# A recurrent step whose f gate takes the two halves of h in separate products

## The reference, cut to what matters

```
xW = einsum('ntd,dk->tnk', x, Wx) + b
def step(carry, xw_t):
    prev_h, prev_c = carry
    a = xw_t + prev_h @ Wh
    i = sigmoid(a[:, 0:Hdim]);          f = sigmoid(a[:, Hdim:2 * Hdim])
    o = sigmoid(a[:, 2 * Hdim:3 * Hdim]); g = tanh(a[:, 3 * Hdim:4 * Hdim])
    next_c = f * prev_c + i * g
    next_h = o * tanh(next_c)
    return (next_h, next_c), next_h
```

## Time and profile before

| what | value |
|---|---|
| time, median of 3 runs | 1904.62 us (1903.64 to 1904.72) |
| time of the profiled execution | 1905.15 us |
| its span, first to last instruction | 1903.0 us |
| TensorE clock granted, mean over the span | 0.626 of full |
| start of the first recurrent step | 468 us |
| last step alone from about | 1590 us |
| busy: TensorE, VectorE, ScalarE, GpSimd | 64%, 62%, 50%, 21% |

### The profile page before, as it was taken

How to read it: one execution, slowest core, us unless ns; L and a number is a source line. 1 busy time by engine, 2 the same in 40 slices (tenths; PEclk the granted TensorE clock), 3 DMA queues, 4 the chain that set the end, 5 groups by cost and what they waited for, 6 DMA issues and landing times.

```text
span 1903.0 us, 60748 instructions
## 1 busy us (share of the span) xinstructions
PE 1214.6 (64%) x21103; PEld 978.4 (51%) x21103; DVE 1174.1 (62%) x6657; ACT 950.6 (50%) x3287; POOL 404.2 (21%) x802
## 2 busy tenths in 40 slices
PE   4666677176777558867775588677764976444444
PEld 3544445145655445656554466555553665444443
DVE  6456634222777765657777666577776665666665
ACT  0333378234766644556666445466654554333332
POOL 4222234432221131311221312112114130000000
PEclk9667655588555557975555589655555886555555
DMA  8000000000000000000000000000000000000000
GB/s 257 0 0 0 0 1 0 1 1 1 3 0 0 2 3 2 2 25 3 0 1 3 2 2 2 25 2 0 1 2 3 2 2 13 0 0 0 0 0 13
DMA packets 14555, 17.85 MB, mean 9 GB/s; under 512 B 3348, under 2 KB 13208, under 8 KB 14360
## 3 DMA queue, kind: packets, MB, share of 16 engines
q1 hardware_dynamic: 10248, 10.50, 1.7%
q10 hardware_dynamic: 4112, 4.86, 0.9%
HBM read 13.25 MB, written 2.10 MB: 8 GB/s over the span
## 4 chain that ended last, share of the span: by engine, by line
PE 41%; DVE 25%; ACT 14%; issue 11%; POOL 6%; DMA 1%; POOLq 1%; ACTq 1%; DVEq 1%; SPq 0%
PE psum L727 20%; DVE cnew L1275 4%; DVE cadd L1272 4%; ACT tC L973 4%; DVE h L1283 3%; PE psum L701 3%; DVE h L1286 3%; PE psum L710 3%; DVE gO L1269 3%; PE psum L669 3%; POOL sc L226 3%; PE psum L679 2%; PE psum L559 2%; PE psum L596 2%; DVE h L1284 1%
## 5 line engine op out<-in xcount | busy, mean ns | idle before, releaser
L727 PE MATMUL psum<-h,wh 128*128 128x8 f16 x16384 | 514.6, 168 | 437.6 <-DVE h L1286 419.6
L727 PEld LDWEIGHTS psum<-h,wh 128*128 128x128 f16 x16384 | 479.7, 103 | 558.4 <-DVE h L1286 526.1
L967 ACT ACTIVATE tA<-gA 128x16 f32<-128x16 f32 x512 | 110.5, 216 | 474.5 <-DVE gA L1265 473.7
L1265 DVE TENSOR_REDUCE gA<-psum 128x16 f32<-128x32 f32 x512 | 97.4, 190 | 214.2 <-PE psum L727 213.5
L973 ACT ACTIVATE tC<-cnew 128x8 f32<-128x8 f32 x512 | 108.8, 213 | 130.9 <-DVE cnew L1275 87.3
L596 PE MATMUL psum<-qbd,kT 128*128 128x256 f16 x512 | 151.0, 400 | 24.5 <-ACT weights L853 21.5
L1272 DVE SCALAR_TENSOR_TENSOR cadd<-tA 128x8 f32<-128x8 f32 x512 | 126.8, 248 | 52.6 <-ACT tA L967 45.4
L853 ACT ACTIVATE weights<-psum 128x512 f16<-128x512 f32 x256 | 152.1, 594 | 0.0
L1283 DVE TENSOR_TENSOR h<-oU,tC 128x8 f16<-128x8 f32 x512 | 89.2, 174 | 97.1 <-ACT tC L973 96.3
L342 POOL TENSOR_TENSOR weights<-tmp,weights 128x512 f16<-128x512 f32 x64 | 74.0, 1157 | 313.2 <-ACT weights L853 313.2
L611 PEld LDWEIGHTS psum<-vs,weights 128*128 128x128 f16 x2048 | 112.3, 111 | 37.6 <-issue 17.2
(11 more groups left out here) (225 smaller groups left out, 2183.7 us busy)
## 6 DMA issues: line engine op xcount, KB each, us to landing
arena<-in_x_dram SPq DMA_DIRECT2D x4, 512.0 KB, 10.0
wf<-in_L_cond_w_f_dram SPq DMA_DIRECT2D x2, 1024.0 KB, 19.7
xs<-in_x_dram SPq DMA_DIRECT2D x4, 512.0 KB, 5.4
out_dram<-place SPq DMA_DIRECT2D x16, 128.0 KB, 2.1
arena<-in_L_cond_w_ada_dram ACTq DMA_DIRECT2D x1, 1536.0 KB
weights<-in_L_cond_Wh_dram ACTq DMA_DIRECT2D x1, 1024.0 KB, 14.7
gates<-in_L_cond_b_ada_dram ACTq DMA_DIRECT2D x8, 128.0 KB, 15.0
wx<-in_L_cond_Wx_dram SPq DMA_DIRECT2D x1, 1024.0 KB, 21.5
```

What stands on the lines that cost most here:

```text
L727: last = mm(cols, wh16[:, half, kc, (g0 + g) * P:(g0 + g + 1) * P], h16[:, kc, :, :], start=False, stop=g == n - 1 and kc == KD - 1 and ha ...
```

## The change

The high and low parts of h move to a new tile `hl`, in which each stands as the third of three columns, the first two being constants. The F bank gets one column per sequence instead of two. TensorE starts each step as soon as the high part is written: it multiplies it with the f gate's weights (8 matmuls of 4 columns). It then waits for the low part and runs gate A (16 matmuls of 8 columns), the low part's products of f into the same columns (8 of 4 columns), and gate O (8 of 8 columns). Since the F bank now holds finished sums, ScalarE reads it directly, the reduce `gF` goes, and the preload of bank F waits for ScalarE's tanh instead of it. On VectorE, h in fp32 is no longer formed for the low part: a scan over triples computes, from the constants, o, tanh(c) and the high part, first 1, then o, then o times tanh(c) minus the high part. It waits until the high part is written. The output store forms o times tanh(c) itself.

```diff
--- before.py
+++ after.py
@@ -157,18 +157,17 @@
         ot = place[:, B * D:2 * B * D]
         big1 = sb("big1", [P, 8])
 
-        h16 = sb("h16", [P, KD, B, 2], F16)
+        hl = sb("hl", [P, 2, KD, B, 3], F16)
         gA = sb("gA", [P, 16])
-        gF = sb("gF", [P, 8])
         gO = sb("gO", [P, 8])
-        h32 = sb("h32", [P, KD * B])
         tA = sb("tA", [P, 16])
         tO = sb("tO", [P, 8])
-        oU = sb("oU", [P, 8])
+        ot3 = sb("ot3", [P, KD * B, 3])
         cmul = sb("cmul", [P, 8, 3])
         cadd = sb("cadd", [P, 8, 3])
         cnew = sb("cnew", [P, 8, 3])
-        tC = sb("tC", [P, 8])
+        oU, tC = ot3[:, :, 1], ot3[:, :, 2]
+        hcol, hi3, lo3 = hl[:, 0, :, :, 2], hl[:, 0].rearrange("p k b e -> p (k b e)"), hl[:, 1].rearrange("p k b e -> p (k b e)")
         unit = sb("unit", [P, GC])
 
         psum = ctx.enter_context(nc.psum_tensor("psum", [P, 8, 512], F32))
@@ -281,11 +280,11 @@
 
         CHUNK = (0, 1, 6, 7, 2, 3, 4, 5)
         UNIT = (0.5,) * 2 + (1.0,) * 2 + (0.5,) * 4
-        GATE_BANKS = ((pA, 0, 4, "l_A"), (pF, 4, 2, "l_F"), (pO, 6, 2, "l_O"))
-
-        def gate_cols(bk, n, r):
-
-            return bk[:, r * n * B * 2:(r + 1) * n * B * 2].rearrange("p (c e) -> p c e", e=2)
+        GATE_BANKS = ((pA, 0, 4, 2), (pF, 4, 2, 1), (pO, 6, 2, 2))
+
+        def gate_cols(bk, n, e, r):
+
+            return bk[:, r * n * B * e:(r + 1) * n * B * e].rearrange("p (c e) -> p c e", e=e)
 
         WLOADS = 8
         BLOCK_LINKS = 105
@@ -704,29 +703,38 @@
                 if half == 1 and b % 2 == 0:
                     pe_gates_T(n + 1, b + 1)
 
-            def put_gates(bk, g0, n, first):
+            def put_gates(bk, g0, n, e, first):
 
                 part = (xw[:, first:first + ROUND, g0:g0 + n, :] if isinstance(first, int) else xw[:, bass.ds(first, ROUND), g0:g0 + n, :])
-                mm(bk[:, 0:ROUND * n * B * 2].rearrange("p (t c e) -> p t c e", t=ROUND, e=2)[:, :, :, 0], ident[:], part.rearrange("p t g b -> p t (g b)"),
+                mm(bk[:, 0:ROUND * n * B * e].rearrange("p (t c e) -> p t c e", t=ROUND, e=e)[:, :, :, 0], ident[:], part.rearrange("p t g b -> p t (g b)"),
                    start=True, stop=True, skip_group_check=True)
 
             def put_round(m, first):
 
-                for (bk, g0, n, made), read in zip(GATE_BANKS, ("l_gA", "l_gF", "l_gO")):
+                for (bk, g0, n, e), read in zip(GATE_BANKS, ("l_gA", "l_tF", "l_gO")):
                     pe.wait_ge(s[read], m)
-                    put_gates(bk, g0, n, first)
+                    put_gates(bk, g0, n, e, first)
+
+            def gate_products(which, r, h_of):
+
+                bk, g0, n, e = GATE_BANKS[which]
+                for g in range(n):
+                    cols = gate_cols(bk, n, e, r)[:, g * B:(g + 1) * B, :]
+                    for kc in range(KD):
+                        for half in range(2):
+                            last = mm(cols, wh16[:, half, kc, (g0 + g) * P:(g0 + g + 1) * P], h_of(kc),
+                                      start=False, stop=g == n - 1 and kc == KD - 1 and half == 1, skip_group_check=True)
+                return last
 
             def pe_step(m, r, more=True):
 
+                both = lambda kc: hl[:, :, kc, :, 2].rearrange("p e b -> p b e")
+                pe.wait_ge(s["l_hi"], m)
+                gate_products(1, r, lambda kc: hl[:, 0, kc, :, 2])
                 pe.wait_ge(s["l_lo"], m)
-                for bk, g0, n, made in GATE_BANKS:
-                    for g in range(n):
-                        cols = gate_cols(bk, n, r)[:, g * B:(g + 1) * B, :]
-                        for kc in range(KD):
-                            for half in range(2):
-                                last = mm(cols, wh16[:, half, kc, (g0 + g) * P:(g0 + g + 1) * P], h16[:, kc, :, :],
-                                          start=False, stop=g == n - 1 and kc == KD - 1 and half == 1, skip_group_check=True)
-                    last.then_inc(s[made], 1)
+                gate_products(0, r, both).then_inc(s["l_A"], 1)
+                gate_products(1, r, lambda kc: hl[:, 1, kc, :, 2]).then_inc(s["l_F"], 1)
+                gate_products(2, r, both).then_inc(s["l_O"], 1)
                 if r == ROUND - 1 and more:
                     put_round(m, m % (2 * P))
 
@@ -965,12 +973,12 @@
             def act_step(m, i, r):
                 act.wait_ge(s["l_gA"], m)
                 A(tA[:], gA[:], ACT.Tanh, scale=down).then_inc(s["l_tA"], 1)
-                act.wait_ge(s["l_gF"], m)
-                A(cmul[:, :, 1], gF[:], ACT.Tanh, scale=down).then_inc(s["l_tF"], 1)
+                act.wait_ge(s["l_F"], m)
+                A(cmul[:, :, 1], gate_cols(pF, 2, 1, r)[:, :, 0], ACT.Tanh, scale=down).then_inc(s["l_tF"], 1)
                 act.wait_ge(s["l_gO"], m)
                 A(tO[:], gO[:], ACT.Tanh, scale=down).then_inc(s["l_tO"], 1)
                 act.wait_ge(s["l_c"], m)
-                A(tC[:], cnew[:, :, 2], ACT.Tanh, scale=0.5).then_inc(s["l_tC"], 1)
+                A(tC, cnew[:, :, 2], ACT.Tanh, scale=0.5).then_inc(s["l_tC"], 1)
 
             act.wait_ge(s["l_init"], 2)
             for part in range(2):
@@ -1048,7 +1056,11 @@
 
             d.memset(qbd[:], 0.0).then_inc(s["l_init"], 1)
             d.memset(vs[:, :, :, :, HD:HD + 1], V_UP).then_inc(s["l_init"], 1)
-            d.memset(h16[:], 0.0).then_inc(s["l_lo"], 1)
+            d.memset(ot3[:], 0.0).then_inc(s["dinit"], 1)
+            d.memset(hl[:], 0.0).then_inc(s["dinit"], 1)
+            v.wait_ge(s["dinit"], 2)
+            d.memset(hl[:, 0, :, :, 0], -1.0).then_inc(s["l_hi"], 1)
+            v.sem_inc(s["l_lo"], 1)
             d.memset(cmul[:, :, 0], 0.0).then_inc(s["dinit"], 1)
             d.memset(cmul[:, :, 2], 0.5).then_inc(s["dinit"], 1)
             d.memset(cadd[:], 0.0).then_inc(s["dinit"], 1)
@@ -1056,7 +1068,7 @@
             d.memset(kap[:, NT:], 0.0).then_inc(s["dinit"], 1)
             d.memset(kmn[:, NT:], 0.0).then_inc(s["dinit"], 1)
 
-            v.wait_ge(s["dinit"], 6)
+            v.wait_ge(s["dinit"], 8)
             for k in range(NT):
                 if k % B == 0:
                     v.wait_ge(s[f"ld_x{k // B}"], 16)
@@ -1262,11 +1274,9 @@
             def dve_step(m, i, r):
 
                 v.wait_ge(s["l_A"], m)
-                d.tensor_reduce(gA[:], gate_cols(pA, 4, r), axis=AX.X, op=ALU.add).then_inc(s["l_gA"], 1)
-                v.wait_ge(s["l_F"], m)
-                d.tensor_reduce(gF[:], gate_cols(pF, 2, r), axis=AX.X, op=ALU.add).then_inc(s["l_gF"], 1)
+                d.tensor_reduce(gA[:], gate_cols(pA, 4, 2, r), axis=AX.X, op=ALU.add).then_inc(s["l_gA"], 1)
                 v.wait_ge(s["l_O"], m)
-                d.tensor_reduce(gO[:], gate_cols(pO, 2, r), axis=AX.X, op=ALU.add).then_inc(s["l_gO"], 1)
+                d.tensor_reduce(gO[:], gate_cols(pO, 2, 2, r), axis=AX.X, op=ALU.add).then_inc(s["l_gO"], 1)
 
                 v.wait_ge(s["l_tA"], m)
                 d.scalar_tensor_tensor(cadd[:, :, 2], tA[:, 0:8], 1.0, tA[:, 8:16], ALU.add, ALU.mult).then_inc(s["l_ig"], 1)
@@ -1275,19 +1285,17 @@
                 d.tensor_tensor_scan(cnew[:].rearrange("p c e -> p (c e)"), cmul[:].rearrange("p c e -> p (c e)"),
                                      cadd[:].rearrange("p c e -> p (c e)"), 0.0, ALU.mult, ALU.add).then_inc(s["l_c"], 1)
                 v.wait_ge(s["l_tO"], m)
-                d.tensor_scalar(oU[:], tO[:], 1.0, 0.5 * H_UP, ALU.add, ALU.mult).then_inc(s["l_oU"], 1)
+                d.tensor_scalar(oU, tO[:], 1.0, 0.5 * H_UP, ALU.add, ALU.mult).then_inc(s["l_oU"], 1)
                 v.wait_ge(s["l_tC"], m)
                 v.wait_ge(s["l_oU"], m)
-                hi, lo = (h16[:, :, :, half] for half in range(2))
-                by_k = lambda t: t[:].rearrange("p (k b) -> p k b", b=B)
-                d.tensor_tensor(hi, by_k(oU), by_k(tC), ALU.mult).then_inc(s["l_hi"], 1)
-                d.tensor_tensor(h32[:], oU[:], tC[:], ALU.mult).then_inc(s["l_h32"], 1)
-                v.wait_ge(s["l_h32"], m)
-                d.tensor_tensor(lo, by_k(h32), hi, ALU.subtract).then_inc(s["l_lo"], 1)
+                by_k = lambda t: t.rearrange("p (k b) -> p k b", b=B)
+                d.tensor_tensor(hcol, by_k(oU), by_k(tC), ALU.mult).then_inc(s["l_hi"], 1)
+                v.wait_ge(s["l_hi"], m + 1)
+                d.tensor_tensor_scan(lo3, ot3[:].rearrange("p c e -> p (c e)"), hi3, 0.0, ALU.mult, ALU.subtract).then_inc(s["l_lo"], 1)
                 d.tensor_copy(cadd[:, :, 0:2], cnew[:, :, 2:3].to_broadcast([P, KD * B, 2])).then_inc(s["l_cc"], 1)
 
-                d.tensor_copy(hs[:, :, :, i:i + 1] if isinstance(i, int) else hs[:, :, :, bass.ds(i, 1)],
-                              h32[:].rearrange("p (k b o) -> p k b o", b=B, o=1)).then_inc(s["l_hs"], 1)
+                d.tensor_tensor(hs[:, :, :, i:i + 1] if isinstance(i, int) else hs[:, :, :, bass.ds(i, 1)],
```

(7 more changed lines are left out.)

## The result

The changed kernel takes 1945.66 us (median; 1942.58 to 1947.17) where the kernel before takes 1904.13: a ratio of 1.0216, 95% interval 1.0199 to 1.0234. Slower, as forecast, but by 41.5 us and not by 7, and outside the forecast range of 1898 to 1925 us.

What follows compares the result with a forecast made beforehand. The prediction took a chain of hand-overs, no engine above 41% of it, as the bound. Losses of 15.5 and 2 us less a gain of 10.7 made +7 us on the median 1904.62: 1911.5 us, range 1898 to 1925.

Steps and rivals of the forecast that it cites:

- 8 x 0.0274 = 0.22 us of TensorE more: Per step on TensorE: splitting F turns 8 matmuls of 8 columns into 16 of 4, costing 0.22 us more.
- Rival 2: Tail: TensorE, carrying more matmuls, might be granted the higher clock; -13 us over 128 steps, 1899 us together; chance 0.05.
- Low part earlier by 0.035 us: VectorE: the scan ends the low part 0.242 us behind the high one, against 0.277; 10.7 us gained over 305 steps.
- F's first half fits under the scan: Where TensorE is idle: the eight matmuls are done at 0.27 us, gate A can start at 0.29, 0.02 to spare.
- The charge per matmul: TensorE: a matmul of 4 columns is charged the same 0.027 us as one of 8 columns.
- Late steps pay in full: Where TensorE comes late, gate A starts 0.20 to 0.22 us later, reaching the end in full: 74 x 0.21 = 15.5 us.
- Rival 1: Hardly anything is lost where TensorE is late: fewer than 33 of 74 steps pay; 1899 us with 25 paying; chance 0.12.
- Reduce of F gone, worth nothing: In an idle step, dropping F's reduce gains nothing: ScalarE's tanh of f is done 0.11 us before the scan of c.
- The sum: Whole kernel: 15.5 us for late steps plus 2 for 64 steps between, less 10.7 gained, together +7 us.

Runs made afterwards that it cites:

- e1: The changed kernel without the products of h's low half with the f gate's weights in the attention loop's steps; 1920.66 us, ratio 1.0071 to the kernel before.
- e2: The kernel before with 8 unread matmuls of 4 columns more in each step of the attention loop's body; 1919.62 us, ratio 1.0070.
- e8: The changed kernel with TensorE's attention loop of three turns written out as straight code; 1928.28 us, ratio 1.0125 to the kernel before.
- e7: The kernel before with 8 unread matmuls of 4 columns more in each carried step outside the attention loop's body; 1932.09 us, ratio 1.0126.
- e0: The changed kernel run once more, unaltered; 1947.15 us, ratio 1.0209 to the kernel before.
- e3: The changed kernel with F kept whole and its reduce, leaving the low part's scan and the product for hs; 1902.59 us, ratio 0.9983 to the kernel before.
- e5: The changed kernel with F's split and ScalarE's direct read only in the tail's 128 steps, the scan in all; 1901.00 us, ratio 0.9969 to the kernel before.
- e9: As e5, but the tail's step behind each preload keeps F whole with its reduce; 1898.38 us, ratio 0.9966 to the kernel before.

## Why the prediction was wrong

**Where it failed: what the eight matmuls cost.** The prediction charged splitting F with "8 x 0.0274 = 0.22 us of TensorE more", and with nothing else. That term is right for TensorE's own time. Two further prices hang on the same eight.

- *Their instructions.* The attention loop's body grew from 1513 to 1769 profiled instructions. The prediction never asked whether a loop body still fits, nor did a rival. It cost 18.3 us, shown by e1, e2 and e8. The trace of before had a sign of it: ten instruction pieces in 465 to 640 us, none in the last two turns of the loop. Where the limit lies it did not tell. The Trainium skill (Runtime: NRT & Kernel Launch, Instruction fetch mechanics) says that TensorE's store is filled in blocks of 16 KB and that a taken branch to instructions not held waits for a fetch; the traces agree, with pieces of 16 KB and 2.98 us. It gives 2048 instructions for TensorE, by which 1769 would have fitted; here the limit lies between 1513 and 1769 profiled ones, and for this loop the measurement decides. Whether fewer can be used or the body has some 280 that the profile does not list, no run tells.
- *The clock.* Rival 2 let the clock rise in the tail. It did not, it stayed at 0.50; it fell in the carried part instead, which e7 shows to come from added matmuls and e0 to come again. The steps whose clock changed carry 16 to 19 us; less some 4 us for the late ones among them, the clock cost an estimated 13 to 15 us. That a stretch's clock could get worse by more work on TensorE was not among the cases.

**Low part earlier by 0.035 us: right as an interval, too large as a gain.** 0.036 us was measured, but a step gains 0.025 from it (e3), since the high part's operation and the way round take a little longer; that the stores into columns of three are the reason is not shown.

**F's first half fits under the scan: right, but only just**, with 0.007 us to spare against 0.02 forecast. The charge per matmul is right, 0.0267 us for 4 columns as for 8; what the sum left out is that the first matmul behind a wait is followed by the next only after 0.047 us.

**Late steps pay in full: right for most.** Forecast 74 steps at 0.21, 15.5 us. In the trace of the change 64 carried steps at an unchanged clock are over 0.1 us longer, 14.8 us together, and each of the 7 tail steps behind a preload is 0.22 us longer. Rival 1, which needed fewer than 33 to pay, is refuted by this. But they are not quite the steps meant: of the 53 to which TensorE was late before and whose clock is unchanged, 39 pay 0.15 us or more and 14 pay less than 0.06, among them one preload of each block, and 23 others, to which it was not late, are over 0.1 us longer, 5.0 us together.

**Reduce of F gone, worth nothing: wrong.** With ScalarE's direct read it gives 0.02 us a step (e5 against e3). The timeline of the tail step had tanh of f done 0.11 us ahead of the scan, and I took that for idle slack; yet the earlier trace rows has "DVEq L1274 0.6%" in the chain of the tail, the wait for that tanh.

**The sum.** Without jumps and clock the parts are +8.3 in the carried steps, some 4 for the late steps among those whose clock changed, and -4.8 in the tail: about +8 us, where the forecast had +7. That this comes so close is partly luck, as the tail gained 2 us more than forecast and the carried part lost 2 to 3 us more. The two terms that were not written down, jumps and clock, are about 33 us.

## What to carry to other kernels

Before making a loop body longer, even by instructions that hide completely, look at the instruction queue while the loop turns: if no pieces come in, the body is being held, and there is something to lose; written out as straight code the same steps lost nothing here (e8). Work that is hidden where an engine waits is paid in full where that engine is late, so put such a split only into the steps that wait (e5, e9). And where a stretch has the higher clock only part of the time, small matmuls added to it can cost more through the clock than through their own time.

## What the runs showed of the hardware that was not expected

- A jump back to instructions no longer held: TensorE's matmuls sit idle for 3.2 to 3.8 us behind it in the change and in e0, instead of 0.6, some 3 us of the chain for each jump; a second idle time of 1.3 to 1.9 us a step later takes the place of a wait of 1.5 us for VectorE. Bodies of 1513 profiled instructions of TensorE showed none of it, 1769 showed it at each jump, 1641 at four of six.
- The first matmul behind a semaphore wait is followed by the next after 0.046 to 0.049 us, and all later ones at 0.027, in the tail steps of every kernel here; so each wait set into a run of matmuls costs 0.02 us, where it falls on the path.
- With 61 to 88 us more of busy time on TensorE in the same 1190 us (e7 and the change), the higher clock was granted for 37 and 27 us less.
- ScalarE's tanh of 8 columns takes 0.163 us from PSUM and 0.213 from SBUF.
